# Sums of both attention layers: one-hots from a TensorE product of bit codes and one relu, in place of four Abs operations and a relu

## The chip, the core and the metric

The kernel runs on one core of a Trainium2 chip. The core has TensorE (matrix products, PE in the profile), VectorE (DVE), ScalarE (ACT), GpSimd (POOL) and SyncE (SP), which here only issues transfers. Each engine takes its own instructions in order and they meet through semaphores. The metric is device time in microseconds (us), as the median of several runs.

## The reference, cut to what matters

A graph of 6250 nodes with 106250 edges sorted by target `dst`, and four layers on it: a two-layer GATv2 attention network, two GCN-like convolutions and an edge network. The change touches the two attention layers:

```
def _gatv2_layer(x, src, dst, Wl, bl, Wr, br, att, bias, heads, out_ch, concat):
    xl = (x @ Wl + bl).reshape(N, heads, out_ch)
    xr = (x @ Wr + br).reshape(N, heads, out_ch)
    e = jax.nn.leaky_relu(xl[src] + xr[dst], NEG_SLOPE)
    logits = jnp.einsum('ehc,hc->eh', e, att)
    m = jax.ops.segment_max(logits, dst, num_segments=N)
    ex = jnp.exp(logits - m[dst])
    denom = jax.ops.segment_sum(ex, dst, num_segments=N)
    alpha = ex / denom[dst]
    msg = xl[src] * alpha[..., None]
    out = jax.ops.segment_sum(msg, dst, num_segments=N)
    ...
h = _gatv2_layer(x, src, dst, Wl1, ..., heads=8, out_ch=16, concat=True)    # layer 1: width 128
h = _gatv2_layer(h, src, dst, Wl2, ..., heads=1, out_ch=64, concat=False)   # layer 2: width 64
```

`segment_sum` over the edges of a target node is what the changed stage computes.

## The kernel before

Edges are cut into 880 tiles of 128, each belonging to one block of 128 target nodes; four tiles are a group, 220 groups in all. A sum over edges is a product: a one-hot matrix (edge by local target number) times the edges' rows. `LOCAL` holds each edge's local number, 0 to 127; an edge of another block has a number outside and must get a row of zeros.

Each attention layer (`gat_layer`) runs these stages, with a barrier of all engines behind each: `two_dense` (projections), `gat_logits` (POOL gathers four tiles a group into a ring of 12 groups, the logits are worked out, rows and logits are kept in DRAM), `edge_max` (running maxima) and `gat_sums`. Beside them POOL sends `merge` transfers, which fill an adjacency matrix for later layers; it issues a stated number of groups (`MERGES`) within each stage, so a barrier also waits for those.

`gat_sums` goes through the groups in a software pipeline written as a list of pieces with delays (`pipeline`, L120); it is unrolled, each engine gets its pieces in the order of the list, and rings of four slots (`RING`) and pairs of PSUM banks tie the engines to each other. For a group q:

- SP issues `fetch_max` (L2221: in layer 1 four transfers of 8 rows, in layer 2 one) and `fetch_rows` (L2230: the kept rows and logits). Before each it waits until its slot is free and increments a semaphore (`settle`).
- PE turns the maxima (`turn_max`, L2239), DVE subtracts them from the logits (`less_max`, L2270), ACT takes Exp (`exps`, L2255), DVE multiplies rows by it in two halves (`first_rows`, `last_rows`, L2282) and puts in the maximum of each segment's first edge (`first_max`, L2274).
- ACT makes the one-hots: `hots` (L2250) takes |row number - LOCAL| for each of four tiles, and at the end of `exps` (L2257) one Relu makes 1 - |.| of all four.
- PE multiplies (`products`, L2304: four f32 products, 144 columns wide), and DVE adds each into its block's accumulator (`Adder.tile`, L1151), interleaved with its other pieces.

Of the kernel before, what the change touches and what calls it, by code (L numbers as in the profile page):

```python
# [7 lines left out]
ALU = mybir.AluOpType  # L8
# [11 lines left out]
P = 128  # L20
# [7 lines left out]
GT = 4  # L28
# [21 lines left out]
UNITS = -(-NB // CB)  # L50
ABLK = 64
SPARE = ABLK - 1

CYCLE = NB - 1
LIGHT = 15
# [63 lines left out]
def pipeline(nc, pieces):  # L119


    most = max(late for _, late in pieces)

    def step(turn, u):
        for piece, late in pieces:
            slot = (u - late) % RING
            own = turn + (u - late - slot) // RING
            q = own * RING + slot
            if isinstance(q, int) and not 0 <= q < GROUPS:
                continue  # L130
            piece(q, slot, own)

    for t in range(GROUPS + most):
        step(t // RING, t % RING)


def gnn(nc, A, out):
    S = Sems(nc)
    ve, ac, pe, po, sp = nc.vector, nc.scalar, nc.tensor, nc.gpsimd, nc.sync
    with ExitStack() as ctx:  # L140
        def sb(name, shape, dt=F32):
            return ctx.enter_context(nc.sbuf_tensor(name, shape, dt))

        def dram(name, shape, dt=F32):
            return nc.dram_tensor(name, shape, dt).ap()
# [31 lines left out]
        CLASH = sb("CLASH", [1, FAR], I32)  # L177
        GIVEN = sb("GIVEN", [1, CYCLE], I32)
        zeros = sb("zeros", [P, CB * P])

        G = sb("G", [P, RING, GT, D + H1])
        OH = sb("OH", [P, 2, GT, P])
# [47 lines left out]
        def go(eng, f, by=1):  # L230
            chain[0].run(eng, f, by=by)
# [19 lines left out]
        def settle(eng, name):  # L251

            eng.sem_inc(S(f"settled_{name}"), 1)
# [12 lines left out]
        def fill(count, eng=ac):  # L266

            for _ in range(count):
                c, f = units_left.pop(0)
                w = min(CB, HEAVY - c * CB) * P  # L270
                eng.dma_start(adj[c, :, f * FILL:(f + 1) * FILL, 0:w],
                             zeros[:, 0:w].unsqueeze(1).broadcast_to([P, FILL, w])).then_inc(filled, 16)
# [17 lines left out]
            end()  # L290


        def sort_edges():

            begin()
# [15 lines left out]
                             ).then_inc(S("edges_copied"), 16)  # L311
            sp.wait_ge(chain[0].sem, chain[0].n)
            fill(FIRST[0], sp)
            go(ve, lambda: ve.tensor_copy(here[0:EP, 0:EC], here_i))
            go(ve, lambda: ve.tensor_copy(after[0:EP, 0:EC], after_i))

# [429 lines left out]
        def places_in_adjacency():  # L746

            begin()
            dst_c, bits = TOTAL[:, :].bitcast(I32), LATER[:, :].bitcast(I32)

            def put(source, right, keep, left):

                go(ve, lambda: ve.tensor_scalar(bits, source, right, keep, ALU.logical_shift_right, ALU.bitwise_and))
                go(ve, lambda: ve.tensor_scalar(bits, bits, left, None, ALU.logical_shift_left))
                go(ve, lambda: ve.tensor_tensor(PLACE[:, :], PLACE[:, :], bits, ALU.bitwise_or))

            wide_bits = (CB * P).bit_length() - 1
# [5 lines left out]
            clashes()  # L763
            ve.wait_ge(chain[0].sem, chain[0].n)

        def mean_and_root(halves, less_mean, root):
# [1080 lines left out]
        def gat_logits(tab, XR, H, C, half):  # L1847
# [30 lines left out]
            with ExitStack() as ps:  # L1878
# [173 lines left out]
                ve.wait_ge(S("masked"), 1)  # L2052
                if not half:
                    places_in_adjacency()
                pipeline(nc, [(gather_rows, 0), (fetch_locals, 0), (fetch_keys, 0), (fill_one, 0), (turned_hots, HOTS_LATE),
                              (pick, PICK_LATE), (add_rows, BEND_LATE), (scale_down, BEND_LATE), (twins, BEND_LATE),
                              (leaky, BEND_LATE), (weigh, BEND_LATE), (add_up, BEND_LATE), (turn_logits, TURN_LATE),
# [3 lines left out]
                po.wait_ge(S("aside"), 4)  # L2061
                po.wait_ge(filled, 16 * (len(UNIT_LIST) + 1 + HEAVY))
                merge(MERGES[half][0])
                for s in range(DEEP):
                    sp.wait_ge(S(f"kept{s}"), 16 * (-(-(GROUPS - s) // DEEP)))
                for s in range(LD):
# [130 lines left out]
        def gat_sums(acc, H, C, weights):  # L2197
# [13 lines left out]
            DIF = BUF[2][:, at + RING:at + 2 * RING, 0:TH].rearrange("p r (t h) -> p r t h", h=H)  # L2211
            by_group = head_d[0:H * TILES * P].rearrange("(h g t e) -> g t h e", h=H, t=GT, e=P)
            whole, R, LOGIT = ring(W, H)
            with ExitStack() as ps:
# [27 lines left out]
                def by_head(a):  # L2242
                    return a.rearrange("p (t h) -> p t h", h=H)

                def hots(q, slot, turn):
# [13 lines left out]

                def weight_column(q, slot, turn):  # L2260
                    if weights:
# [690 lines left out]
```

## Time and profile before

| | us |
|---|---|
| median of three runs (6759.13 to 6762.62) | 6760.27 |
| span of the profiled execution | 6773.4 |
| ... logits of layer 1, in that execution | 173 to 1280 |
| ... sums of layer 1 | 1426 to 1906 |
| ... sums of layer 2 | 3156 to 3567 |

Over the span PE is busy 71%, DVE 62%, ACT 32%, POOL 68%, but each stage has its own limit: in the chart of 40 slices, of 169 us each, ACT shows 8 and 9 tenths in the slices that lie within the sums of layer 1 and 9 in those of layer 2, against 4 or less in most others. The profile's chain of waits covers the last 1400 us alone, so the two stages have to be read from their timelines. Busy times of instructions that follow each other closely overlap: a rate is better read from the starts of two equal instructions in two turns of the loop.

### The profile page before, as it was taken

To read this page: it belongs to the slowest core of one execution; us is meant where nothing else is said; L and a number is where in the kernel's file an instruction comes from. 1 tells how busy PE (TensorE), PEld (TensorE's weight loads), DVE (VectorE), ACT (ScalarE), POOL (GpSimd) and SP (SyncE) were. 2 spreads that over 40 slices of the span, in tenths; PEclk is the share of its full clock that TensorE was granted. 3 is DMA by queue.
4 is the path that set the end of the run, shared out by engine and by line. 5 is a ranking of instruction groups with operands and counts; after the bars stand their busy time and mean duration, and the time that the engine had idled before them with its cause. 6 is when DMAs were issued, how large, how long until landed. Compare 5 with 4: busy or idle time off the path is not lost. (4 is left out here: it accounts for less than half of the span.)

```text
span 6773.4 us, 97374 instructions
## 1 busy us (share of the span) xinstructions
PE 4805.9 (71%) x22507; PEld 3515.7 (52%) x22507; DVE 4202.7 (62%) x13908; ACT 2200.1 (32%) x5456; POOL 4572.6 (68%) x4354
## 2 busy tenths in 40 slices
PE   3777765248776666443886996555555699999998
PEld 2444443136664444333776995555555455555555
DVE  7899985588976666335886445555555644344343
ACT  4444444268943333334993003111111300000000
POOL 1777777778857777777876662777777177276473
PEclk8555555578965555556998997776777799999999
DMA  5988865557744444333445884555555299899997
GB/s 202 305 285 290 275 184 146 111 101 138 144 80 106 107 106 99 81 80 47 76 76 151 286 284 137 156 152 150 150 151 149 58 299 306 289 304 295 299 305 256
DMA packets 896445, 1222.20 MB, mean 180 GB/s; under 512 B 229324, under 2 KB 633952, under 8 KB 882906
## 3 DMA queue, kind: packets, MB, share of 16 engines
q1 hardware_dynamic: 585406, 877.15, 40.3%
q0 software_dynamic: 206208, 217.12, 16.4%
q10 hardware_dynamic: 104268, 121.66, 5.4%
q8 instruction: 202, 3.31, 0.2%
q14 instruction: 361, 2.96, 0.1%
HBM read 979.26 MB, written 237.38 MB: 180 GB/s over the span
## 5 line engine op out<-in xcount | busy, mean ns | idle before, releaser
L1121 POOL DMA_INDIRECT ACC<-table,TABS x1760 | 1661.5, 944 | 610.1 <-issue 610.1
L1436 POOL DMA_INDIRECT BUF<-table,TABS x840 | 796.5, 948 | 600.7 <-issue 245.4
L1202 POOL DMA_INDIRECT adjacency<-TABS x600 | 964.1, 1607 | 305.5 <-issue 265.5
L1739 POOL DMA_INDIRECT TABS<-table,SPOT_SRC x836 | 841.1, 1006 | 317.8 <-issue 317.8
L1912 PE MATMUL picked<-BUF,G 128*128 x2368 | 597.0, 434 | 425.5 <-DVE ACC L1937 399.7
L1912 PEld LDWEIGHTS picked<-BUF,G 128*128 128x128 f32 x2368 | 527.0, 328 | 667.9 <-issue 667.9
L2304 PE MATMUL asum<-BUF 128*128 128x144 f32 x3520 | 563.5, 305 | 165.4 <-DVE BUF L2282 163.3
L1762 PE MATMUL pre<-wmat,BUF 128*128 128x128 f32 x1672 | 342.6, 369 | 469.5 <-DVE BUF L1772 435.8
L1920 DVE TENSOR_TENSOR picked<-picked,ACC 128x512 f32<-128x512 f32 (+1 forms) x440 | 247.6, 563 | 580.0 <-DMA ACC<-table,TABS 526.8
L2304 PEld LDWEIGHTS asum<-BUF 128*128 128x128 f32 x3520 | 478.5, 198 | 196.2 <-issue 179.3
L2250 ACT ACTIVATE BUF<-iota_row,TABS 128x128 f32<-128x128 f32 x1760 | 555.2, 386 | 23.0 <-PEq L95 23.0
L1762 PEld LDWEIGHTS pre<-wmat,BUF 128*128 128x128 f32 x1672 | 295.4, 266 | 514.3 <-issue 478.9
L1925 ACT ACTIVATE BUF<-picked 128x512 f32<-128x512 f32 (+1 forms) x440 | 215.6, 490 | 959.3 <-DVE picked L1920 958.8
L1151 DVE TENSOR_TENSOR ACC<-ACC,asum 128x144 f32 (+1 forms) x1760 | 462.0, 263 | 95.5 <-PE asum L2304 15.4
L1778 ACT ACTIVATE BUF<-BUF 128x512 f32<-128x512 f32 x209 | 131.8, 630 | 968.8 <-DVE BUF L1772 968.8
L1772 DVE TENSOR_TENSOR BUF<-pre,TABS 128x512 f32<-128x512 f32 x209 | 144.5, 691 | 485.8 <-DMA TABS<-table,SPOT_SRC 452.1
L1912 PE MATMUL picked<-BUF,OH 128*128 x1152 | 290.7, 434 | 215.4 <-DVE ACC L1937 215.4
L1912 PEld LDWEIGHTS picked<-BUF,OH 128*128 128x128 f32 x1152 | 256.5, 328 | 333.3 <-issue 333.3
L1567 DVE TENSOR_TENSOR BUF<-BUF,turned 128x128 f32 x560 | 161.0, 287 | 396.5 <-PE turned L1473 330.5
L1350 PE MATMUL sums<-ACC,BUF 128*128 128x128 f32 x3332 | 386.1, 276 | 23.1 <-DMA BUF<-adjacency 13.3
L1978 PE MATMUL wspread<-BUF,ones 1*128 1x512 f32 x300 | 306.2, 1122 | 123.6 <-DVE BUF L1999 114.2
L1350 PEld LDWEIGHTS sums<-ACC,BUF 128*128 128x128 f32 x3332 | 379.4, 193 | 24.8 <-DMA BUF<-adjacency 13.8
(431 smaller groups left out, 9802.7 us busy)
## 6 DMA issues: line engine op xcount, KB each, us to landing
TABS<-adjacency SPq DMA_DIRECT2D x272, 512.0 KB
BUF<-in_edge_pair SPq DMA_DIRECT2D x836, 128.0 KB
BUF<-adjacency SPq DMA_DIRECT2D x102, 1024.0 KB
BUF<-adjacency SPq DMA_DIRECT2D x204, 512.0 KB
adjacency<-zeros ACTq DMA_DIRECT2D x44, 1792.0 KB
G<-adjacency SPq DMA_DIRECT2D x136, 512.0 KB
kept<-ACC SPq DMA_DIRECT2D x220, 272.0 KB, 4.8
G<-kept SPq DMA_DIRECT2D x220, 272.0 KB
```

The costliest lines, as they stand in the source:

```text
L1121: po.indirect_dma_start(rows[:, slot, j, 0:width], None, tab, bass.IndirectOffsetOnAxis(ap=SRC[:, q * GT + j:q * GT + j + 1], axis=0)).the ...
L1151: ve.tensor_tensor(at, at, self.from_[:, j, 0:self.width], ALU.add).then_inc(S("added"), 1)
L1202: po.indirect_dma_start(adj_flat, bass.IndirectOffsetOnAxis(ap=PLACE[:, k:k + 1], axis=0), TOTAL[:, k:k + 1], None, compute_op=ALU.add).th ...
L1350: m = pe.matmul(sums[:, j, 0:P], RA[n % len(RA)][:, (i * w + j) * P:(i * w + j + 1) * P], xw[:, b + i, :], start=b + i == 0, stop=b + i == ...
L1436: po.indirect_dma_start(R[:, q % deep_ring, j, :], None, table, bass.IndirectOffsetOnAxis(ap=SRC[:, k:k + 1], axis=0)).then_inc(S(f"gather ...
L1739: po.indirect_dma_start(R[:, g % RD, j, :], None, table, bass.IndirectOffsetOnAxis(ap=SPOT_SRC[:, k:k + 1], axis=0)).then_inc(S(f"gathered ...
L1762: m = pe.matmul(pre[g % FREE][:, j, :], PAIR[:, g % PD, j, 0:D], wmat[:, :], start=True, stop=True)
L1912: m = pe.matmul(z, OHT[q % HD][:, j, :], XR[:, bass.ds(blocks[j], 1), 0:W].rearrange("p a d -> p (a d)"), start=True, stop=True)
L1920: ve.tensor_tensor(z, z, whole[:, q % DEEP, 0:GT * W], ALU.add).then_inc(S("summed"), 1)
L1978: pe.matmul(wspread[n % 2][:, :, :].rearrange("p t e -> p (t e)"), ones[P // 4 * (n % KD):P // 4 * (n % KD) + 1, :], WROW[n % KD].rearrang ...
L2250: ac.activation(HOT[:, slot, j, :], iota_row[:, :], ACT.Abs, scale=-1.0, bias=LOCAL[:, bass.ds(q * GT + j, 1)]).then_inc(S("gap"), 1)
L2304: m = pe.matmul(sums[slot % 2][:, j, 0:WIDE], HOT[:, slot, j, :], RHS[:, slot, j, :], start=True, stop=True)
```

## The change

Each edge's local number is turned once into a code of 8 values: seven of -0.5 or 0.5 for its bits and one that is -6 for an edge of this block and -16 otherwise. Each column has a code of seven times -2 or 2, and 1. The product of an edge's and a column's code is 7 - 6 = 1 where they agree, at most -1 where a bit differs, and negative for edges outside; a relu of it is the one-hot. A group of four tiles is one bf16 product: 32 rows of codes against a fixed 32 x 512 matrix (`COLUMNS`, four copies of the columns' codes on the diagonal).

```
+        CODES = sb("CODES", [P, 3, TTAB], BF16)
+        COLUMNS = sb("COLUMNS", [P, GT, P], BF16)
+        code_d = dram("codes", [TTAB, BITS, P], BF16)
...
+        def code_columns():            # in sort_edges, ahead of the first work on the loaded edges
+            ...
+            for b in range(BITS - 2, -1, -1):
+                own.run(ve, lambda: ve.tensor_scalar(bits[:, b:b + 1], left, float(P // 2), 0.5, ALU.is_ge, ALU.subtract))
+                own.run(ve, lambda: ve.scalar_tensor_tensor(left, bits[:, b:b + 1], -float(1 << b), left, ALU.mult, ALU.add))
+            ...
+                for t in range(GT):
+                    own.run(pe, lambda: pe.matmul(columns[0:CODE_ROWS, t, :], apart[:, t * CODE_ROWS:(t + 1) * CODE_ROWS],
+                                                  ident[:, :], start=True, stop=True))
+                own.run(ve, lambda: ve.tensor_copy(COLUMNS[0:CODE_ROWS, :, :], columns[0:CODE_ROWS, :, :]))
...
+        def codes_of_locals(left):     # in gat_logits of layer 1, ahead of its pipeline
+            rows = local_d.rearrange("(g p) e -> p g e", p=P)
+            sp.dma_start(left.rearrange("p (g e) -> p g e", g=TCOL), rows).then_inc(S("local_rows"), 16)
+            ...
+            for n, b in enumerate(range(BITS - 2, -1, -1)):
+                room = n % 3
+                if n > 1:
+                    ve.wait_ge(S(f"codes_stored{room}"), 16 * ((n + 1) // 3))
+                go(ve, lambda: ve.tensor_scalar(CODES[:, room, :], left, float(P // 2), 0.5, ALU.is_ge, ALU.subtract))
+                ...
+                if b:
+                    go(ve, lambda: ve.scalar_tensor_tensor(left, CODES[:, room, :], -float(1 << b), left, ALU.mult, ALU.add))
+            for b in stores:
+                ...
+                sp.dma_start(code_d.rearrange("(g p) b e -> b p g e", p=P)[b],
+                             CODES[:, room, :].rearrange("p (g e) -> p g e", g=TCOL)).then_inc(S(f"codes_stored{room}"), 16)
...
         # gat_sums
+                meets = [psum(ps, f"meets{i}", [P, GT, P]) for i in range(2)]
+                def fetch_codes(q, slot, turn):
+                    wait(sp, S("met"), q - CD + 1)
+                    settle(sp, "sync")
+                    sp.dma_start(coded[:, q % CD, :], code_d[q * GT:(q + 1) * GT].rearrange("t b e -> (t b) e")
+                                 ).then_inc(S(f"codes{q % CD}"), 16)
+                def meet(q, slot, turn):
+                    pe.wait_ge(S(f"codes{q % CD}"), 16 * (q // CD + 1))
+                    wait(pe, S("hot"), q - 1)
+                    pe.matmul(meets[slot % 2][:, :, :].rearrange("p t d -> p (t d)"), coded[:, q % CD, :],
+                              COLUMNS[0:CODE_ROWS, :, :].rearrange("p t d -> p (t d)"), start=True, stop=True
+                              ).then_inc(S("met"), 1)
                 def hots(q, slot, turn):
+                    ac.wait_ge(S("met"), q + 1)
                     wait(ac, S("summed"), q - RING + 1)
-                    for j in range(GT):
-                        ac.activation(HOT[:, slot, j, :], iota_row[:, :], ACT.Abs, scale=-1.0,
-                                      bias=LOCAL[:, bass.ds(q * GT + j, 1)]).then_inc(S("gap"), 1)
+                    ac.activation(HOT[:, slot], meets[slot % 2][:, :, :], ACT.Relu).then_inc(S("hot"), 1)
                 def exps(q, slot, turn):
                     ac.wait_ge(S("dif"), q + 1)
                     ac.activation(RHS[:, slot, :, W:W + H], DIF[:, slot], ACT.Exp).then_inc(S("exp"), 1)
-                    ac.wait_ge(S("gap"), (q + 1) * GT)
-                    ac.activation(HOT[:, slot], HOT[:, slot], ACT.Relu, scale=-1.0, bias=1.0
-                                  ).then_inc(S("hot"), 1)
...
-                pipeline(nc, [(fetch_max, 0), (fetch_rows, 1), (turn_max, 2), (ve_step(less_max), 2),
+                pipeline(nc, [(fetch_max, 0), (fetch_codes, 0), (fetch_rows, 1), (turn_max, 2), (meet, 2),
+                              (ve_step(less_max), 2),
                               (ve_step(first_rows), 3), (ve_step(first_max), 2), (ve_step(last_rows), 3),
                               (ve_step(weight_column), 2), (add, 5),
-                              (flush, 0), (hots, 2), (exps, 2), (products, 4)])
+                              (flush, 0), (exps, 2), (hots, 2), (products, 4)])
```

SP's queue in the middle of the sums of layer 1, before; L2227 is `fetch_max` and L2233 `fetch_rows`, and `pool` numbers are semaphores:

```order
L2233 DMA G<-kept 128x544 [waits pool6]
L2227 DMA BUF<-heads 8x128 [waits pool2]
L2227 DMA BUF<-heads 8x128 x3
L2233 DMA G<-kept 128x544 [waits pool6]
L2227 DMA BUF<-heads 8x128 [waits pool2]
L2227 DMA BUF<-heads 8x128 x3
```

And now, with L2293 and L2299 the same two pieces and L2315 `fetch_codes`:

```order
L2299 DMA G<-kept 128x544 [waits pool9]
L2293 DMA BUF<-heads 8x128 [waits pool2]
L2293 DMA BUF<-heads 8x128 x3
L2315 DMA CODES<-codes 32x128 [waits pool5]
L2299 DMA G<-kept 128x544 [waits pool9]
L2293 DMA BUF<-heads 8x128 [waits pool2]
L2293 DMA BUF<-heads 8x128 x3
L2315 DMA CODES<-codes 32x128 [waits pool5]
```

Each turn of the loop has a sixth transfer with a wait of its own, between the maxima and the rows.

PE's queue in the same place, before; `asum` is the product of one-hots and rows, `mcol` the turned maxima:

```order
L2239 MATMUL mcol_27<-ident,BUF 128x32 [waits pool10,pool16]
L2304 MATMUL asum_29<-BUF 128x144 [waits pool10,pool19,pool6,pool15]
L2304 MATMUL asum_29<-BUF 128x144 x3
L2239 MATMUL mcol_26<-ident,BUF 128x32 [waits pool10,pool4]
L2304 MATMUL asum_28<-BUF 128x144 [waits pool10,pool19,pool6,pool15]
```

And now, with L2305, L2322 and L2380 for `turn_max`, `meet` and `products`:

```order
L2305 MATMUL mcol_30<-ident,BUF 128x32 [waits pool14,pool19]
L2322 MATMUL meets_28<-COLUMNS,CODES 128x512 [waits pool15,pool27]
L2380 MATMUL asum_32<-BUF 128x144 [waits pool14,pool24,pool9,pool15]
L2380 MATMUL asum_32<-BUF 128x144 x3
L2305 MATMUL mcol_29<-ident,BUF 128x32 [waits pool14,pool4]
L2322 MATMUL meets_27<-COLUMNS,CODES 128x512 [waits pool15,pool6]
```

One product of 512 columns stands between the turned maxima and the four products of each group.

## Rows read from the trace of the kernel before

**Rows 1.** Busy time of each engine (and instructions) in the two sums stages

```profile
core 0: us, PE busy (x) PEld busy (x) DVE busy (x) ACT busy (x) POOL busy (x), PEclk, DMA share, GB/s
...
1426.00:1906.00 480.00, 370.38 (x2200) 318.30 (x2200) 434.11 (x1761) 422.79 (x1321) 361.62 (x224) 0.93 0.68 137
...
3156.00:3567.00 411.00, 338.78 (x2200) 293.84 (x2200) 341.62 (x1982) 402.74 (x1320) 325.73 (x208) 0.99 0.48 74
```

**Rows 2.** Timeline, one turn of the sums of layer 1: start, duration, engine

```profile
1649.11 0.30 DVE L1151 TENSOR_TENSOR ACC<-ACC,asum 128x144 f32 x1
...
1649.27 0.34 SPq L2233 DMA_DIRECT2D G<-kept  x1
1649.28 1.22 PE L2304 MATMUL asum<-BUF 128*128 128x144 f32 x8 [0.47 <-DVE BUF L2282]
...
1649.54 0.23 ACT L2255 ACTIVATE BUF<-BUF 128x32 f32<-128x32 f32 x1
...
1649.72 1.28 SPq L2227 DMA_DIRECT2D BUF<-heads  x4
...
1650.20 1.26 ACT L2250 ACTIVATE BUF<-iota_row,TABS 128x128 f32<-128x128 f32 x4
...
1650.43 0.40 PE L2239 MATMUL mcol<-ident,BUF 32*128 32x32 f32 x2
...
1651.12 0.30 DVE L1151 TENSOR_TENSOR ACC<-ACC,asum 128x144 f32 x1
...
1651.28 0.34 SPq L2233 DMA_DIRECT2D G<-kept  x1
```

**Rows 3.** Timeline, SP's queue at the start of the same stage

```profile
1426.31 2.84 SPq L2227 DMA_DIRECT2D BUF<-heads  x8
...
1429.71 1.28 SPq L2227 DMA_DIRECT2D BUF<-heads  x4
1431.10 0.34 SPq L2233 DMA_DIRECT2D G<-kept  x1
1431.55 1.28 SPq L2227 DMA_DIRECT2D BUF<-heads  x4
```

**Rows 4.** Timeline, SP's queue: a slow issue, and the last turns

```profile
1626.29 2.85 SPq L2227 DMA_DIRECT2D BUF<-heads  x4
...
1891.73 2.54 SPq L2233 DMA_DIRECT2D G<-kept  x2
```

**Rows 5.** Timeline, turns of the sums of layer 2

```profile
3401.10 1.22 PE L2304 MATMUL asum<-BUF 128*128 128x144 f32 x8 [0.42 <-DVE BUF L2282]
3401.18 0.22 DVE L1151 TENSOR_TENSOR ACC<-ACC,asum 128x67 f32 x1
...
3401.49 0.19 ACT L2255 ACTIVATE BUF<-BUF 128x4 f32<-128x4 f32 x1
...
3402.25 0.38 PE L2239 MATMUL mcol<-ident,BUF 4*128 4x4 f32 x2
...
3402.89 0.23 DVE L1151 TENSOR_TENSOR ACC<-ACC,asum 128x67 f32 x1
...
3403.33 0.19 ACT L2255 ACTIVATE BUF<-BUF 128x4 f32<-128x4 f32 x1
```

**Rows 6.** Timeline, POOL behind the barrier that ends the sums of layer 2

```profile
3569.20 1.56 POOL L1202 DMA_INDIRECT adjacency<-TABS  x1 [22.15 <-issue]
```

**Rows 7.** Timeline, SP's queue at the start of the sums of layer 2

```profile
3158.16 0.26 SPq L2224 DMA_DIRECT2D BUF<-heads  x1
```

**Rows 8.** Timeline, PE in a later stage: f32 products of 512 columns

```profile
5451.38 3.60 PE L1519 MATMUL sums<-BUF,ACC 128*128 128x512 f32 x8
```

**Rows 9.** Timeline, DVE in `sort_edges`: its first work on loaded edges

```profile
14.30 0.60 DVE L314 CAST BUF<-BUF 125x850 f32<-125x850 int32 x1 [9.56 <-DMA BUF<-in_dst]
```

**Rows 10.** Timeline, start of the logits of layer 1

```profile
173.36 0.95 POOL L1121 DMA_INDIRECT ACC<-table,TABS  x1 [69.70 <-issue]
...
175.45 1.09 DVE L755 TENSOR_TENSOR TABS<-TABS 128x896 int32<-128x896 int32 x1
...
184.09 0.20 DVE L1186 TENSOR_TENSOR GIVEN<-st 1x48 int32<-1x48 f32 x1
...
199.18 1.02 SPq L2038 DMA_DIRECT2D kept<-ACC  x1
```

More of the change, by code:

```diff
@@ L52 @@
 SPARE = ABLK - 1
+BITS = 8
+CODE_ROWS = GT * BITS
+CD = 8
 CYCLE = NB - 1
@@ L290, in constants @@
             end()
+        def code_columns():
+            own = Chain(S("columns"))
+            room = G[:, 0, :, :].rearrange("p t d -> p (t d)")
+            left, bits, apart = room[:, 0:1], room[:, 8:8 + BITS], room[:, 64:64 + GT * CODE_ROWS]
+            own.run(ve, lambda: ve.tensor_copy(left, iota_col[:, :]))
+            own.run(ve, lambda: ve.memset(bits, 0.0))
+            for b in range(BITS - 2, -1, -1):
+                own.run(ve, lambda: ve.tensor_scalar(bits[:, b:b + 1], left, float(P // 2), 0.5, ALU.is_ge, ALU.subtract))
+                own.run(ve, lambda: ve.scalar_tensor_tensor(left, bits[:, b:b + 1], -float(1 << b), left, ALU.mult, ALU.add))
+            own.run(ve, lambda: ve.tensor_scalar(bits, bits, 4.0, None, ALU.mult))
+            own.run(ve, lambda: ve.memset(bits[:, BITS - 1:BITS], 1.0))
+            own.run(ve, lambda: ve.memset(apart, 0.0))
+            for t in range(GT):
+                at = t * (CODE_ROWS + BITS)
+                own.run(ve, lambda: ve.tensor_copy(apart[:, at:at + BITS], bits))
+            with ExitStack() as ps:
+                columns = psum(ps, "columns", [P, GT, P])
+                for t in range(GT):
+                    own.run(pe, lambda: pe.matmul(columns[0:CODE_ROWS, t, :], apart[:, t * CODE_ROWS:(t + 1) * CODE_ROWS],
+                                                  ident[:, :], start=True, stop=True))
+                own.run(ve, lambda: ve.tensor_copy(COLUMNS[0:CODE_ROWS, :, :], columns[0:CODE_ROWS, :, :]))
         def sort_edges():
@@ L313, in sort_edges @@
             fill(FIRST[0], sp)
+            code_columns()
             go(ve, lambda: ve.tensor_copy(here[0:EP, 0:EC], here_i))
@@ L763, in places_in_adjacency @@
             clashes()
+            ve.wait_ge(chain[0].sem, chain[0].n)
+        def codes_of_locals(left):
+            rows = local_d.rearrange("(g p) e -> p g e", p=P)
+            sp.dma_start(left.rearrange("p (g e) -> p g e", g=TCOL), rows).then_inc(S("local_rows"), 16)
+            ve.wait_ge(S("local_rows"), 16)
+            after, valid = CODES[:, 0, :], CODES[:, 1, :]
+            go(ve, lambda: ve.tensor_scalar(after, left, 0.0, None, ALU.is_ge))
+            go(ve, lambda: ve.scalar_tensor_tensor(valid, left, float(P), after, ALU.is_lt, ALU.mult))
+            go(ve, lambda: ve.tensor_scalar(CODES[:, 2, :], valid, 10.0, -16.0, ALU.mult, ALU.add))
+            made = {BITS - 1: (2, chain[0].n)}
+            stores = [BITS - 1]
+            for n, b in enumerate(range(BITS - 2, -1, -1)):
[3 more added lines that the diff above has]
+                go(ve, lambda: ve.tensor_scalar(CODES[:, room, :], left, float(P // 2), 0.5, ALU.is_ge, ALU.subtract))
+                made[b] = (room, chain[0].n)
+                stores.append(b)
+                if b:
+                    go(ve, lambda: ve.scalar_tensor_tensor(left, CODES[:, room, :], -float(1 << b), left, ALU.mult, ALU.add))
+            for b in stores:
+                room, known = made[b]
+                sp.wait_ge(chain[0].sem, known)
+                settle(sp, "sync")
+                sp.dma_start(code_d.rearrange("(g p) b e -> b p g e", p=P)[b],
+                             CODES[:, room, :].rearrange("p (g e) -> p g e", g=TCOL)).then_inc(S(f"codes_stored{room}"), 16)
             ve.wait_ge(chain[0].sem, chain[0].n)
@@ L2054, in gat_logits @@
                     places_in_adjacency()
+                    codes_of_locals(JUNK[:, :, :, :].rearrange("p r t d -> p (r t d)")[:, 0:TTAB])
                 pipeline(nc, [(gather_rows, 0), (fetch_locals, 0), (fetch_keys, 0), (fill_one, 0), (turned_hots, HOTS_LATE),
@@ L2063, in gat_logits @@
                 merge(MERGES[half][0])
+                if not half:
+                    for room, stores in enumerate((3, 2, 3)):
+                        sp.wait_ge(S(f"codes_stored{room}"), 16 * stores)
                 for s in range(DEEP):
@@ L2213, in gat_sums @@
             whole, R, LOGIT = ring(W, H)
+            coded = CODES[:, :, :].rearrange("p r e -> p (r e)")[0:CODE_ROWS, 0:CD * P].rearrange(
+                "p (r e) -> p r e", r=CD)
             with ExitStack() as ps:
+                meets = [psum(ps, f"meets{i}", [P, GT, P]) for i in range(2)]
                 mcol = [psum(ps, f"mcol{i}", [P, 4 * P]) for i in range(2)]
@@ L2243, in by_head @@
                     return a.rearrange("p (t h) -> p t h", h=H)
+                def fetch_codes(q, slot, turn):
+                    wait(sp, S("met"), q - CD + 1)
+                    settle(sp, "sync")
+                    sp.dma_start(coded[:, q % CD, :], code_d[q * GT:(q + 1) * GT].rearrange("t b e -> (t b) e")
[6 more added lines that the diff above has]
+                              ).then_inc(S("met"), 1)
                 def hots(q, slot, turn):
+                    ac.wait_ge(S("met"), q + 1)
                     wait(ac, S("summed"), q - RING + 1)
-                    for j in range(GT):
-                        ac.activation(HOT[:, slot, j, :], iota_row[:, :], ACT.Abs, scale=-1.0,
-                                      bias=LOCAL[:, bass.ds(q * GT + j, 1)]).then_inc(S("gap"), 1)
+                    ac.activation(HOT[:, slot], meets[slot % 2][:, :, :], ACT.Relu).then_inc(S("hot"), 1)
                 def exps(q, slot, turn):
```

## The prediction

> **What bounds the kernel now.** The profile's chain of waits ends in the last layer and says nothing of these stages, so I took the busy times by stage first and then one turn of each loop. In the sums of layer 2 ACT is busy 402.7 of 411 us, in those of layer 1 422.8 of 480, where DVE has 434.1 [rows 1]. The reader is to see from the timeline which engine has no gap in a turn, by the distance between equal instructions.
>
> Layer 2: ACT's Exp starts at 3401.49 and again at 3403.33, a turn of 1.84 us. DVE's turn is shorter: its first add of a group starts at 3401.18 and 3402.89, which is 1.71 [rows 5]. It runs on until one of its multiplications finds the Exp not ready. So ACT sets the pace of layer 2.
>
> Layer 1: equal DVE adds stand at 1649.11 and 1651.12, a turn of 2.01 us that DVE fills with eight pieces; ACT (0.66 from Exp over Relu to the first Abs, then four Abs) needs the same 1.84 and so has 0.17 to spare; PE starts its products after a gap of 0.47 [rows 2]. DVE sets the pace, ACT only nearly. The third engine close to it is SP, which no busy time shows. Its own turn, when nothing holds it, is 1.84: from 1429.71 over 1431.10 to 1431.55 [rows 3], of which 1.28 are the four issues of maxima and 0.34 the issue of the rows. In the steady loop SP's turn is 2.01 as well (1649.27 to 1651.28), and from the end of its maxima (1649.72 + 1.28 = 1651.00) to the next rows 0.28 pass, against 0.11 when free [rows 2, 3]. SP's slack is thus 0.17 us in a turn, no more. The average turn of the stage is longer than the steady one: (1891.73 - 1426.31) / 219 = 2.12 [rows 3, 4]. Part is PE at half clock in short stretches (granted clock 0.93 over the stage [rows 1]), and part is slow issues on SP, such as four maxima in 2.85 instead of 1.28 [rows 4]; I count 34 turns with such an issue, together 14 us over the usual.
>
> **The change, part by part.** *ACT*, both layers: four Abs go, 1.84 - 0.66 = 1.18 of a turn [rows 2, 5], and a Relu of 128 x 512 stays, now from PSUM. ACT's turn falls to about 0.7. In layer 1 this was hidden behind DVE's 2.01 and is worth nothing in itself. In layer 2 it lifts the bound.
>
> *DVE* in the loops: no instruction comes or goes. Its turns of 2.01 and 1.71 stay.
>
> *SP* in the loops: one more transfer in each turn, of 32 rows of 256 bytes. Issues near it: 0.26 for 4 rows [rows 7], 0.32 for each of the four of 8 rows (1.28 / 4), 0.34 for the rows of a group, which fill 128 partitions [rows 3]. I take 0.31, bounds 0.26 and 0.34. It has a wait and a `settle` ahead, which cost 0.11 where the same pair stands today. So 0.42, bounds 0.37 and 0.46. In layer 2 SP needs 0.26 + 0.34 + 0.42 + two gaps of 0.11, or 1.24, and stays hidden. In layer 1 it needs 1.84 + 0.42 = 2.26, which is more than DVE's 2.01: SP becomes the bound. 219 turns of 2.26 are 495 us. The slow issues no longer hide in slack: 14 us, with six transfers for five some 16. 511 in place of 465.4, thus +46 us; the half clock of PE, which is now absorbed by rings that stay ahead, is the reason why I don't add its cost again. With the bounds of the issue +35 and +55. The tail behind the last transfer gets shorter by about 1 us, since the others follow SP closer: +45.
>
> The Trainium skill says in "Trainium Kernel Development and Optimization", Key Constraints, that issuing transfers from several engines only saves the sequencer's issue time, since all run on the same DMA engines. By that rule an added transfer of 8 KB costs this kernel its issue alone, and the sum above is of the right kind; the trace agrees in that the DMA share is 0.68 in this stage, not full [rows 1].
>
> *PE* in the loops: one bf16 product of 512 columns and 32 rows for each group. The trace has no bf16 product. From below, one of the eight records of a group's products, 144 columns, takes 0.14 (eight records fill the 1.15 from 3401.10 to 3402.25 [rows 5]). From above, an f32 record of 512 columns takes 0.43 (two starts 3.43 apart make eight; 3.60 with the last one's drain [rows 8]). I take 0.26, between them and nearer to the lower, since an f32 record of the same columns moves twice the bytes. Layer 1: turned maxima from 1650.43 to 1650.83, then a gap to 1651.29 [rows 2]; 0.26 fits in its 0.47, and even 0.43 does. In layer 2 PE has 1.15 for products and some 0.30 for the turned maxima, so 1.71 with the new product: level with DVE's 1.71. Together I take 1.75.
>
> The Trainium skill, "TensorE: Matmul & The Clock Gate", section Back-to-back issue gap, puts a bf16 product at one cycle for each column, 0.21 us for 512 at 2.4 GHz. An estimate by that page is a PE turn of 1.66 and a layer 2 bound by DVE at 1.71. No row here shows it.
>
> *Layer 2 as a whole*: 220 turns of 1.84 become 220 of 1.75, or 20 us less. But POOL has its own work in this stage, its 208 merge transfers [rows 1], and a barrier waits for it. It idles 22.15 us before its first transfer behind the barrier, some 2 of them the crossing [rows 6]; so no more than 20 can be won, whatever the engines do. Both limits lie close together, so I take -16, bounds -20 and, with a product of 0.43 and a PE turn of 1.88, +10.
>
> *`code_columns`*: about 27 small operations on DVE, each waiting for the one before, four products and a copy, all ahead of the cast that waits 9.56 us for loaded edges [rows 9]. I estimate 8 us, from the 0.2 to 0.25 that dependent small operations take at a time (L1186 and its neighbours [rows 10]) and some 0.7 for each product: hidden, +0 to +2 us; I take +1.
>
> *`codes_of_locals`*: 16 operations of 896 columns, at most 1.09 each [rows 10], behind the places (end 184.3), and waits for rooms that are still being stored; about 20 us, and SP's queue holds its first fetches of locals behind the stores of the codes. All of the logits' loop starts 20 us later, but POOL sets that stage: one gather each 1.25 us, 12 groups ahead, so it meets a full ring only at 173.4 + 48 x 1.25 = 233. The first `kept` is issued at 199.2 [rows 10] and would be at about 220, landing by 225. Nothing is lost; the cover is gone if the delay exceeds 30 us.
>
> *Sum*: +45 - 16 + 1 + 0 = +30 us, on the profiled execution's 6773.4 us of span 6803. That execution is 13 us above the median of the runs, which is no part of these stages that I can name, so I put the difference on the median: 6790 us.
>
> **The rivals.**
> *A, SP has room.* The new issue might be cheaper than its neighbours, or overlap with its wait, and SP's turn stay under 2.01. For it: SP waits in most turns today. Against it: its slack is 0.17 and the cheapest issue in reach is 0.26 without its wait. Then layer 1 stays as it is, perhaps a few us better where ACT's lag behind the half clock goes, and layer 2 gives its 16: 6760 - 16 + 1 = 6745, faster.
> *B, PE becomes the bound of layer 2.* If the new product costs 0.43 as the f32 record does, PE's turn there is 1.88 and layer 2 gains nothing but loses 10; layer 1 still pays 45: 6760 + 45 + 10 + 1 = 6816. It decides from 0.39 upwards (1.15 + 0.30 + 0.39 = 1.84). For it: `meet` is in order ahead of the products. Against it: bf16.
> *C, the new start of the logits isn't hidden.* DMA share is high there, the stores of the codes have small rows, and each third one is waited for. If the delay is 50 us instead of 20, POOL stands still for 20: 6810.
> *D, PE falls to half clock in layer 1 more often.* It idles 2.26 - 1.15 - 0.30 - 0.26 = 0.55 of a turn, as today (2.01 - 1.15 - 0.30 = 0.56), and today most of the stage is granted 2.4 GHz (0.93 [rows 1]). At 1.2 GHz its turn would be twice 1.71, or 3.4 us; a fifth of the turns there adds 0.2 x 219 x 1.1, some 50: 6840.
>
> **How the numbers follow.** Forecast 0.58, A 0.16, B 0.12, C 0.08, D 0.06. The forecast's own range is 6772 (issue 0.26, layer 2 at -20, slow issues half absorbed) to 6808. Down to A's 6745 and up past B's 6816 to 6824 the range leaves out the better half of A and most of D. A measurement of this kernel tells no less than 0.2%, or 13.5 us, from no change. Faster by more than that: most of A, 0.14. Same: the rest of A and the lower edge of the forecast, 0.12. Slower: 0.74.
>
> **What would show it.** Right: in the sums of layer 1 equal issues of the rows on SP stand 2.26 apart, with no gap in SP's turn longer than 0.12, and DVE waits for the DMA of kept rows or maxima in each turn; the stage ends some 45 us later. In layer 2 the turn is 1.71 to 1.76, ACT is busy under half of it, and POOL's idle time before the barrier is 2 to 6 us in place of 22. The product of codes takes 0.2 to 0.3. DVE's cast of loaded edges still starts at 14 to 16, and POOL's gathers in the logits stay 1.25 apart. Wrong: SP still waits for DVE in layer 1 (A), PE without a gap in layer 2 (B), a gap between gathers near 233 (C), a granted clock under 0.85 in layer 1 (D).

## The result and the profile after

The changed kernel takes 7295.4 us (median of 4 runs, 7291.2 to 7306.9) against 6760.7 for the kernel before on the same chip: the ratio is 1.079 [1.078, 1.081]. The prediction was 6790 with a range to 6824. The direction was right, the size wrong by more than ten times: +535 us in place of +30.

Both stages that the change touches grew, and nothing else did. The length of a stage is taken from DVE's clearing of the accumulator to DVE's first instruction behind the stage.

| us | before | after |
|---|---|---|
| start of the sums of layer 1 | 1427.8 | 1431.2 |
| sums of layer 1 | 478.4 | 714.2 |
| between the two sums | 1251.5 | 1251.8 |
| sums of layer 2 | 410.2 | 704.9 |
| behind them, to the end of the span | 3205.5 | 3190.0 |

The last line holds nothing that was changed; its 15 us come for the most part from the profiled execution of before, 13 us over the median, in which this part is the longest; in those of all other kernels below it takes 3187 to 3200. Busy times of the same stages in the kernel after, which answer to [rows 1]:

```profile
core 0: us, PE busy (x) PEld busy (x) DVE busy (x) ACT busy (x) POOL busy (x), PEclk, DMA share, GB/s
1431.00:2145.00 714.00, 704.35 (x2420) 541.60 (x2420) 446.61 (x1761) 157.68 (x440) 351.32 (x224) 0.50 0.46 95
3397.00:4102.00 705.00, 699.09 (x2420) 542.63 (x2420) 331.08 (x1982) 160.84 (x440) 325.62 (x208) 0.50 0.29 46
```

Read the third number from the right first: the granted clock is 0.50, that is 1.2 GHz, from end to end in both stages. It was 0.93 and 0.99. PE is busy 704 of 714 us and 699 of 705: it sets the pace of both layers. ACT's busy time did fall, from 423 and 403 to 158 and 161, and is worth nothing. In the middle of the stages, where no start and no end is counted in, PE has no gap at all:

```profile
1500.00:1800.00 300.00, 300.00 (x1030) 230.42 (x1030) 187.17 (x749) 67.08 (x188) 251.10 (x161) 0.50 0.55 96
3500.00:3800.00 300.00, 300.00 (x1040) 232.60 (x1038) 140.87 (x846) 68.75 (x188) 239.88 (x154) 0.50 0.38 47
```

PE's part of the timeline in layer 1, to be held against [rows 2]:

```profile
1702.31 0.63 PE L2305 MATMUL mcol<-ident,BUF 32*128 32x32 f32 x2
1702.76 0.61 PE L2322 MATMUL meets<-COLUMNS,CODES 32*128 32x512 bf16 x1
1703.30 2.29 PE L2380 MATMUL asum<-BUF 128*128 128x144 f32 x8
1705.52 0.63 PE L2305 MATMUL mcol<-ident,BUF 32*128 32x32 f32 x2
1705.96 0.61 PE L2322 MATMUL meets<-COLUMNS,CODES 32*128 32x512 bf16 x1
```

From one pair of turned maxima to the next are 3.21 us: 0.45 turned maxima, 0.54 codes, 2.22 products. Before, the same group's products took 1.15 from start to start and the turn was 2.01. The new product is only 0.54 of the 1.20 us by which the turn grew; the rest is the old work at half clock. Layer 2 has the same turn: its products start at 3600.03 and 3603.21.

```profile
3600.03 2.29 PE L2380 MATMUL asum<-BUF 128*128 128x144 f32 x8
...
3602.86 0.23 DVE L1210 TENSOR_TENSOR ACC<-ACC,asum 128x67 f32 x1 [1.57 <-PE asum L2380]
3603.00 0.15 DVE L2346 TENSOR_TENSOR BUF<-G,mcol 128x4 f32<-128x4 f32 x1
3603.18 0.21 ACT L2334 ACTIVATE BUF<-BUF 128x4 f32<-128x4 f32 x1 [2.45 <-DVE BUF L2346]
3603.21 1.09 PE L2380 MATMUL asum<-BUF 128*128 128x144 f32 x3
```

DVE waits 1.57 for the products and ACT 2.45 for DVE; PE waits for nobody. 219 turns of 3.2 are 701 us, nearly the whole of the 705 and 714 that the stages take.

The rest of the prediction can be read off as well. SP's free turn at the start of layer 1 (against [rows 3]), from one issue of rows to the next:

```profile
1436.10 0.36 SPq L2299 DMA_DIRECT2D G<-kept  x1
1436.56 1.28 SPq L2293 DMA_DIRECT2D BUF<-heads  x4
1437.94 0.31 SPq L2315 DMA_DIRECT2D CODES<-codes  x1
1438.36 0.36 SPq L2299 DMA_DIRECT2D G<-kept  x1
```

It is 2.26, as computed, with the new issue at 0.31. At a PE turn of 3.2 it doesn't matter.

### The profile page after: what moved, and what is told of

It is laid out like the page before. It is cut to its first block and busy times, and to the rows that moved or that the text cites. A ratio compares the mean times of both kernels' runs of the same rounds, so it can differ in the third digit from the quotient of the medians.

```text
span 7292.1 us, 98323 instructions
## 1 busy us (share of the span) xinstructions
PE 5487.1 (75%) x22955; PEld 3979.7 (55%) x22955; DVE 4220.1 (58%) x13948; ACT 1694.4 (23%) x3696; POOL 4563.0 (63%) x4354
## 5 line engine op out<-in xcount | busy, mean ns | idle before, releaser
L2380 PE MATMUL asum<-BUF 128*128 128x144 f32 x3520 | 1004.1, 467 | 2.7 <-DVE BUF L2358 1.6
L2380 PEld LDWEIGHTS asum<-BUF 128*128 128x128 f32 x3520 | 852.6, 330 | 199.3 <-issue 196.8
L1313 POOL DMA_INDIRECT G<-table,TABS x280 | 275.6, 984 | 130.4 <-issue 96.6
```

The costliest lines, as they stand in the source:

```text
L1313: po.indirect_dma_start(R[:, q % RING, j, :], None, table, bass.IndirectOffsetOnAxis(ap=SRC[:, q * GT + j:q * GT + j + 1], axis=0)).then_i ...
L2380: m = pe.matmul(sums[slot % 2][:, j, 0:WIDE], HOT[:, slot, j, :], RHS[:, slot, j, :], start=True, stop=True)
```

## The experiments

A product's rows are here those over which it sums, 32 for the codes; in a profile line they are the first number of `32*128`. Theory: an added product that has few rows holds TensorE at 1.2 GHz, whatever its busy time. The rivals are that the product costs its time and PE is simply full; that the clock needs a better start; and that SP's added transfer does the harm. The table has all runs; "clock" is the mean of the whole execution (0.745 in the profiled one of before), the lengths are those of the profiled execution. Each ratio is to runs of the kernel before on the same chip, whose medians lie between 6755.4 and 6765.8. "One run" is a single execution; 15 executions of the kernel before, in one series, spread over 22 us, so a single run tells 7284 from 6746 but not 6770 or 6746 from 6760.

| kernel | us | ratio to before | clock | sums 1 | sums 2 |
|---|---|---|---|---|---|
| before | 6760.7 | | 0.745 | 478.4 | 410.2 |
| after | 7295.4 | 1.079 [1.078, 1.081] | 0.675 | 714.2 | 704.9 |
| rows128 | 6810.5 | 1.008 [1.006, 1.009] | 0.749 | 540.7 | 397.2 |
| before_x32 | 7284.4 | one run | 0.676 | 713.2 | 703.8 |
| before_x64 | 7329.4 | one run | 0.677 | 735.5 | 723.2 |
| before_x72 | 6746.3 | one run | 0.749 | 461.3 | 410.4 |
| before_x96 | 6750.5 | one run | 0.753 | 462.0 | 410.3 |
| before_x128 | 6746.1 | one run | 0.751 | 463.4 | 410.3 |
| before_x128_timed | 6745.2 | 0.998 [0.997, 0.999] | 0.749 | 461.2 | 410.3 |
| before_x32c128 | 7156.4 | one run | 0.675 | 642.8 | 634.0 |
| before_f32x32 | 7366.5 | one run | 0.673 | 747.9 | 744.2 |
| before_x32small | 6770.0 | one run | 0.745 | 478.0 | 410.3 |
| warm | 6999.6 | one run | 0.712 | 717.3 | 402.6 |
| before_fetch | 6821.4 | 1.009 [1.007, 1.010] | 0.742 | 533.5 | 410.3 |
| act_fetch | 6739.6 | 0.996 [0.995, 0.997] | 0.753 | 461.0 | 395.5 |
| hybrid | 6734.5 | 0.995 [0.994, 0.997] | 0.751 | 462.5 | 395.7 |

**rows128.** The changed kernel with the same product over all 128 rows; the rows from 32 on are zeros in both operands.

```
-pe.matmul(meets[slot % 2]..., coded[:, q % CD, :], COLUMNS[0:CODE_ROWS, :, :]...)
+pe.matmul(meets[slot % 2]..., coded_all[:, q % CD, :], COLUMNS[:, :, :]...)
```

> The changed kernel, but the product of codes takes all 128 rows: the rows 32 to 127 of both operands are zeros, so it computes the same. Theory 1 (rows): TensorE's clock stays at 1.2 GHz because the product of 32 rows keeps TensorE busy for long and counts for little; with 128 rows the clock rises to 2.4 GHz some 10 us into each sums stage, as in the kernel before, and the time is what I forecast with a 2.4 GHz clock, 6770 to 6810. Theory 2 (any product): every further product of 512 columns in the turn does it, whatever its rows: 7295, granted clock 0.50 in both stages. Theory 3 (other parts of the change: new waits on SP and ACT): 7295 too.

Zeros in 96 rows win 485 us, and theories 2 and 3 fall. The 6810.5 lie at the upper edge of what theory 1 was given. The busy times by stage:

```profile
1434.00:1975.00 541.00, 444.96 (x2420) 346.67 (x2420) 440.44 (x1762) 158.52 (x440) 353.18 (x224) 0.91 0.62 125
3230.00:3627.00 397.00, 386.13 (x2418) 317.40 (x2417) 333.51 (x1983) 152.76 (x440) 325.34 (x208) 0.98 0.52 82
```

The clock is nearly back at what it was. Layer 2 is now shorter than before by 13.0; layer 1 is longer by 62.3, for the most part the term of SP (below).

**before_x32 and before_x128.** The kernel before with one more bf16 product in each turn, behind the turned maxima, of 32 or of 128 rows and 512 columns; nothing reads its result.

```
+def extra_product(q, slot, turn):
+    pe.matmul(extra...[:, 0:512], source[0:32, 0:P], source[0:32, 512:512 + 512], start=True, stop=True)
```

> The kernel before with one bf16 product of 32 rows and 512 columns more in each turn of both sums stages, behind the turned maxima; it waits for nothing, nobody waits for it, and its result isn't used. Theory 1 (rows) and theory 2 (any product): the clock stays at 1.2 GHz, the turn is 3.2 us in layer 1 and 3.0 or more in layer 2, in all 7230 to 7300. Theory 3 (the new waits or transfers): clock as before, layer 1 as before, layer 2 0 to 10 us longer, 6760 to 6775.

> The same as before_x32 with 128 rows in the added product. Theory 1: the clock rises as in the kernel before, perhaps with fewer falls in layer 1; 6750 to 6775. Theory 2: as before_x32, 7230 to 7300. Theory 3: 6760 to 6775.

> The kernel before with an unused bf16 product of 128 rows x 512 columns in every turn, timed this time. One look gave 6746 us with both stages at 2.4 GHz nearly throughout, layer 1's sums in 463.4 us in place of 478.4, layer 2's unchanged at 410.3. If the removal of the clock's dips in layer 1 is real, the ratio is 0.998 (about -14 us) and the interval ends below 1.000; if the dips were chance of one execution, the ratio is 1.000 and layer 1 as long as in the kernel before.

PE's timeline of before_x32 in layer 1:

```profile
1700.45 2.29 PE L2310 MATMUL asum<-BUF 128*128 128x144 f32 x8
1702.67 0.63 PE L2241 MATMUL mcol<-ident,BUF 32*128 32x32 f32 x2
1703.12 0.61 PE L2245 MATMUL extra<-beyond 32*128 32x512 bf16 x1
1703.66 0.61 PE L2310 MATMUL asum<-BUF 128*128 128x144 f32 x1
```

This is the turn of the changed kernel to the hundredth, with all the Abs operations, without a transfer of codes, without a code table. The product alone carries the loss. With 128 rows the same product makes the kernel not slower but a little faster (before_x128_timed, 0.998).

**before_x64, before_x96, before_x72.** The same with other numbers of rows (`source[0:64, ...]` and so on).

> The kernel before with the unused product over 64 rows (512 columns). Theory 1 (rows): somewhere between 32 rows (clock stays at 1.2 GHz, 7284) and 128 rows (6746). If only rows beside the work already there matter, at 1.2 GHz the turn is 3.2 us as with 32 rows, and the result shows on which side 64 rows fall: about 6750, or about 7284, or layer 2 alone at 2.4 GHz, about 6990.

> The kernel before with an unused bf16 product of 96 rows x 512 columns in every turn of both sums. 32 and 64 rows held TensorE at 1.2 GHz (7284 and 7329 us), 128 rows held it at 2.4 GHz (6746 us). If only products that fill the array's rows count: 0.50 in both stages and about 7300 us. If the rows add up, three quarters of them should be enough for most of the time: over 0.8 and under 6900 us. I hold the second slightly more likely.

> The kernel before with an unused bf16 product of 72 rows x 512 columns in every turn of both sums. 64 rows gave 7329 us at 1.2 GHz, 96 rows 6750 us at 2.4 GHz. If the switch lies between what fits in half the array's rows and what doesn't: 72 rows behave as 96 do, both stages at 1.00, 6740 to 6760 us. If the rows count by their number and the switch lies somewhere between 64 and 96: mixed or 0.50, over 6900 us. I hold the first at 60 in 100.

One stretch of layer 1 from each of 64 and 72 rows:

```profile
1500.00:1800.00 300.00, 300.00 (x997) 229.66 (x997) 181.69 (x728) 174.06 (x545) 250.60 (x160) 0.50 0.53 91
```

```profile
1500.00:1800.00 300.00, 274.41 (x1612) 208.29 (x1613) 283.45 (x1172) 280.71 (x879) 250.93 (x155) 1.00 0.73 146
```

Eight rows more, and 583 us less. In 300 us PE does 1612 pieces of work in place of 997 and still has 26 us to spare. (The 45 us between 32 and 64 rows are a turn of 3.31 in place of 3.21, at the same clock.) The Trainium skill, "TensorEngine Tiling (Array Packing)", Performance Considerations, names row tiling for a contraction of at most 64 rows: two row tiles at 64, four at 32. The switch that these runs show lies between 64 and 72 rows, where that use ends; that the tiling is its cause no run shows.

**before_x32c128, before_f32x32, before_x32small.** What else about the product matters: a bf16 product of 32 rows with 128 columns, an f32 product of 32 rows and 128 columns, and a bf16 one of 32 rows and 4 columns.

```
x32c128:  source[0:32, 0:P] by source[0:32, 512:512 + 128]      (bf16)
f32x32:   beyond[0:32, 0, :] by beyond[0:32, 1, :]              (f32, 128 columns)
x32small: source[0:32, 0:P] by source[0:32, 512:512 + 4]        (bf16)
```

> The kernel before with an unused bf16 product of 32 rows and only 128 columns in every turn of both sums, so a quarter of the length of the product that by itself took the kernel to 7284 us. If it is the mere presence of a product with few rows that holds TensorE at 1.2 GHz: granted clock 0.50 in both stages, some 7150 to 7250 us. If it is the share of time spent in such products (32 rows x 512 columns were 0.60 us of a 3.2 us turn; these would be 0.15 of 2.8 at 1.2 GHz): the clock stays mostly at 2.4 GHz, perhaps with more dips than in the kernel before (0.91 in layer 1), 6750 to 6850 us.

> The kernel before with an unused f32 product of 32 rows x 128 columns in every turn of both sums, which takes TensorE about as long as a bf16 product of 512 columns. The kernel before has four f32 products of 4 rows and 4 columns in every turn (turned maxima) and yet reaches 2.4 GHz, so few rows alone are not enough for the loss. If few rows over many columns do it whatever the type: granted clock 0.50, some 7280 us. If it is the bf16 type together with few rows: the clock stays at about 0.9 to 1.0, 6740 to 6800 us.

> The kernel before with an unused bf16 product of 32 rows x 4 columns in every turn of both sums. 128 columns gave 7156 us and 512 columns 7284 us, both at 0.50 throughout. If any bf16 product of few rows holds the clock down: 0.50 in both stages, some 7100 us. If it takes a certain share of columns: the clock is that of the kernel before, 0.91 and more, 6750 to 6790 us. I hold the second at 60 in 100, since the four f32 products of 4 x 4 do no harm.

One stretch of each layer, first of before_x32c128, then of before_f32x32, then of before_x32small, whose second stretch is an earlier one because its layer 2 ends at 3570:

```profile
1500.00:1800.00 300.00, 300.00 (x1145) 256.31 (x1145) 207.66 (x833) 199.18 (x625) 251.32 (x156) 0.50 0.58 104
3500.00:3800.00 300.00, 300.00 (x1156) 258.67 (x1155) 156.78 (x945) 198.69 (x630) 177.68 (x114) 0.50 0.33 49
```

```profile
1500.00:1800.00 300.00, 300.00 (x1071) 255.29 (x1069) 178.46 (x712) 170.82 (x535) 250.71 (x161) 0.50 0.53 89
3500.00:3800.00 300.00, 300.00 (x1071) 255.13 (x1070) 132.62 (x804) 168.79 (x536) 251.23 (x161) 0.50 0.37 41
```

```profile
1500.00:1800.00 300.00, 236.16 (x1551) 205.35 (x1551) 274.55 (x1131) 270.65 (x849) 252.25 (x156) 0.94 0.71 141
3200.00:3500.00 300.00, 254.81 (x1806) 220.84 (x1807) 252.27 (x1480) 300.00 (x985) 250.08 (x161) 1.00 0.50 76
```

The type is not it: f32 does the same harm. A fourth of the columns does the same harm too, so for before_x32c128 the first of its two expectations came true and the second, that a short product would be let through, fell. With 4 columns the stages are as before, although TensorE changes from 128 rows to 32 and back just as often: that change by itself does not hold the clock down. The turned maxima of the kernel before had misled me. They are products of few rows too, 32 rows by 32 columns in layer 1 and 4 by 4 in layer 2 (the expectations speak of 4 by 4 alone), and were there all along, at a clock of 0.93 and 0.99.

**warm.** The changed kernel with 12 f32 products of 128 rows and 512 columns ahead of each stage's loop.

```
+for _ in range(12):
+    pe.matmul(meets[1]..., ident[:, :], beyond[:, :, :]..., start=True, stop=True)
```

> The changed kernel with twelve dense f32 products (128 rows, 512 columns, result not used) on TensorE at the start of each sums stage, some 20 us at 1.2 GHz. If the loop only lacks a start (at 2.4 GHz its own turns would keep the clock up), the clock is 0.9 or more in both stages and the time 6790 to 6850. If the loop's mix can't keep the clock (theory 1 in its strict form), it falls back within some us: 7290 to 7330.

Stretches of both stages:

```profile
1430.00:1450.00 20.00, 17.53 (x59) 9.08 (x58) 10.51 (x22) 2.83 (x9) 16.71 (x11) 0.89 0.49 79
1450.00:1500.00 50.00, 49.58 (x175) 38.05 (x174) 32.13 (x130) 11.59 (x34) 41.99 (x27) 0.52 0.60 106
1500.00:1800.00 300.00, 300.00 (x1031) 231.01 (x1030) 187.83 (x750) 67.00 (x187) 251.12 (x161) 0.50 0.56 96
3400.00:3420.00 20.00, 19.56 (x75) 10.84 (x74) 8.65 (x42) 4.04 (x12) 16.65 (x12) 0.90 0.39 57
3500.00:3800.00 300.00, 293.17 (x1867) 227.95 (x1865) 255.19 (x1532) 116.23 (x337) 242.17 (x155) 1.00 0.51 82
```

PE in layer 1 where the clock falls:

```profile
1447.00 0.38 PE L2322 MATMUL meets<-COLUMNS,CODES 32*128 32x512 bf16 x1
1449.43 1.22 PE L2380 MATMUL asum<-BUF 128*128 128x144 f32 x8 [2.06 <-DVE BUF L2358]
...
1451.62 2.26 PE L2380 MATMUL asum<-BUF 128*128 128x144 f32 x8 [0.42 <-DVE BUF L2358]
```

Both layers are started near 2.4 GHz. In layer 1 PE then idles for 2.06 and 0.42 us, waiting for DVE, and at 1451.62 a group's products take 2.26 in place of 1.22: the clock has fallen. It never returns, though PE is busy without a gap from 1500 on. Layer 2 keeps 2.4 GHz to its end, with no wait of PE longer than 0.4 and with the same 32-row product that otherwise holds it at 1.2: for it both clocks are stable, and the start decides. So neither expectation held for both layers, the first came true in layer 2 and the second in layer 1. The few rows do not forbid the clock outright; they keep it from rising. That they also bring it down is not shown: in layer 1 it fell behind a wait, and it falls now and then in the kernel before as well (0.92 from 1500 to 1800), but comes back there. Whether layer 1, whose turned maxima are larger, could keep it without that wait was not tried.

**before_fetch.** The kernel before with the added transfer of 8 KB a turn on SP's queue alone, for a test of my own term.

```
+def fetch_more(q, slot, turn):
+    ...
+    sp.dma_start(FETCHED[0:32, q % 8, :], local_d[q % 27 * 32:q % 27 * 32 + 32])
```

> The kernel before with only the added transfer: in each turn of both sums stages SP fetches 32 rows of 256 bytes more, behind the maxima, with a wait and a settle ahead; nobody uses them. If SP's issue time is the second cost of the change (rows128 took 541 us for the sums of layer 1 against 478), SP's turn is 2.26 to 2.28 with no slack, the stage 530 to 540 us, the sums of layer 2 unchanged at 410, in all 6805 to 6820. If the loss of rows128 in layer 1 came from the product or from the new order on ACT, this runs in 6755 to 6765.

SP's queue in layer 1:

```profile
1697.56 0.35 SPq L2234 DMA_DIRECT2D G<-kept  x1
1698.02 1.28 SPq L2228 DMA_DIRECT2D BUF<-heads  x4
1699.41 0.31 SPq L2246 DMA_DIRECT2D FETCHED<-locals  x1
1699.84 0.35 SPq L2234 DMA_DIRECT2D G<-kept  x1
```

A turn of 2.28 with no gap over 0.12: SP is the bound, as the prediction had it. The stage grew by 55.1 to 533.5, as expected here (the prediction had 45 for this term); layer 2 didn't change. The total of 6821.4 is 1 us over its range.

**act_fetch.** rows128 with the fetch of the codes issued by ACT, which has had time since the Abs operations went.

```
-wait(sp, S("met"), q - CD + 1); settle(sp, "sync");   sp.dma_start(coded[:, q % CD, :], ...)
+wait(ac, S("met"), q - CD + 1); settle(ac, "scalar"); ac.dma_start(coded[:, q % CD, :], ...)
```

> rows128 with the codes' transfer issued by ACT's queue in place of SP's. If SP's issue time is the whole loss of layer 1, its turn goes back to DVE's 2.01 and the stage to 463 to 480 us; layer 2 stays at 397; set-up costs 6 more: in all 6730 to 6750. If ACT's issue delays the Exp that DVE waits for, layer 1 stays above 500 and the total above 6770.

The first expectation came true: layer 1 takes 461.0, 2 under its range, and layer 2 395.5. PE in layer 2:

```profile
3300.47 0.38 PE L2307 MATMUL mcol<-ident,BUF 4*128 4x4 f32 x2
3300.79 0.39 PE L2326 MATMUL meets<-COLUMNS,CODES 128*128 128x512 bf16 x1
3301.04 1.22 PE L2384 MATMUL asum<-BUF 128*128 128x144 f32 x8
3302.18 0.38 PE L2307 MATMUL mcol<-ident,BUF 4*128 4x4 f32 x2
```

**hybrid.** Layer 1 makes its one-hots as before, with an unused full-row product in each turn; layer 2 makes them from the codes over 128 rows.

> Layer 1 with Abs and Relu as in the kernel before, plus one unused bf16 product of 128 rows and 512 columns in each turn; layer 2 with codes over 128 rows. Layer 1 463 us as in before_x128 (the added product keeps the clock at 2.4 GHz), layer 2 397 as in rows128, set-up +6: 6730 to 6745, faster than both kernels. If the gain of before_x128 was chance, layer 1 takes 478 and the total is 6745 to 6755.

Both of the last two beat the kernel before, by 0.4 and 0.5%; their intervals overlap. The gain has two parts that can be told apart. Layer 2 wins 14.7 and 14.5 us by ACT's lifted turn. Layer 1 wins 17.4 and 15.9, which needs no codes: before_x128_timed, with all four Abs in place, wins 17.2 there. The stretch from 1500 to 1800 in the kernel before and in before_x128_timed:

```profile
1500.00:1800.00 300.00, 237.75 (x1400) 204.60 (x1400) 272.41 (x1121) 268.80 (x842) 252.09 (x157) 0.92 0.71 139
```

```profile
1500.00:1800.00 300.00, 274.54 (x1614) 208.37 (x1614) 283.51 (x1173) 280.87 (x880) 252.03 (x155) 1.00 0.72 146
```

The dips of the clock are gone, and DVE, which bounds this stage, gets 1173 instructions through in place of 1121.

## Why the prediction was wrong

**The step that failed** is the one on PE in the loops. For layer 1 it says "0.26 fits in its 0.47, and even 0.43 does", and for layer 2 it gives PE 1.71 with the new product. Every duration in it, that of the old products too ("one of the eight records of a group's products, 144 columns, takes 0.14"), is one at 2.4 GHz, and that the clock stays there rests on nothing but PE's idle time, which rival D found to be as before. At that clock the sizes were right: with 128 rows, in act_fetch, the product takes 0.25 (3300.79 to 3301.04) and PE's turn in layer 2 is 1.71 (3300.47 to 3302.18); with 32 rows, in layer 2 of warm, the turn is 1.72. What the product does to the clock was missing. Measured, the clock is 0.50 and PE's turn 3.21, and this gives +236 in layer 1 and +295 in layer 2 in place of +45 and -16. before_x32, rows128 and the step from 64 to 72 rows show that it is the few rows of the product; why few rows have this effect on the clock no run shows.

**Rival D** had the right mechanism, a fall to half clock, with the wrong driver, place and size. It looked for the cause in the share of time that PE idles, found it unchanged, and priced a fifth of the turns of layer 1 at +50. Its sign, a clock under 0.85 in layer 1, did show. The runs show the contrary: PE idles nowhere and is at 1.2 GHz. A busier engine was granted less. The Trainium skill, "TensorE: Matmul & The Clock Gate", What's actually happening, says that the clock is set by how busy the engine has been, and that sustained work brings 2.4 GHz. Here 300 of 300 busy us at 0.50, for hundreds of us, disagree; the measurement decides.

**The range** was bounded by the nearest rows for the product, 0.14 and 0.43. Both ends came from products of 128 rows, and the new one has 32. The bounds of a new instruction should have covered what it does to its neighbours too.

A row of the kernel before could have raised the doubt. It is from the logits' stage, where products of 1 row and 512 columns take 81.6 of PE's 290.6 busy us. The stretch from 300 to 700, by busy time, and then the row of these products in it:

```profile
300.00:700.00 400.00, 290.59 (x885) 177.19 (x883) 359.56 (x965) 175.33 (x322) 302.31 (x321) 0.50 0.87 288
```

```profile
L1978 PE MATMUL wspread<-BUF,ones 1*128 1x512 f32 x80 | 81.6, 1121 | 46.2 <-DVE BUF L1999 43.3 <-DVE BUF L1995 2.8
```

PE is busy for 73% there and yet at 0.50, while the sums of layer 1 have 370 of 480, 77%, at 0.93 [rows 1]. Whether the thin products are what holds that stage at 1.2 GHz wasn't tried.

**Layer 1 at full clock.** SP as the bound: right (2.26 forecast, 2.26 to 2.28 measured). The stage costs +62 in rows128 and +55 in before_fetch, against +45: about 4 us are the turn of 2.28 (219 x 0.02), the rest of the difference isn't explained by the runs. The clock is 0.84 from 1500 to 1800 in before_fetch, where PE waits more, so its dips are perhaps not absorbed as I took them to be; that is argued, not shown.

**Layer 2 at full clock.** -16 forecast, -13.0 to -14.7 measured. POOL's idle time before the barrier's end falls from 22.15 [rows 6] to 7.52 in act_fetch; I had said 2 to 6.

**`code_columns`.** The cast of loaded edges was the cover:

```profile
14.63 0.60 DVE L344 CAST BUF<-BUF 125x850 f32<-125x850 int32 x1 [1.31 <-DMA BUF<-in_dst]
```

It starts 0.33 later and has waited 1.31 in place of 9.56 [rows 9]: 8.25 us of work hidden, where I had estimated 8. Nothing of it is left where the logits begin: their first gather starts at 173.40 in place of 173.36.

**`codes_of_locals`.** POOL doesn't stand still, so C fell. The first `kept` was forecast at about 220:

```profile
216.60 1.54 SPq L2097 DMA_DIRECT2D kept<-ACC  x1
```

POOL's gathers from 190 to 600 wait 0.3 us for that transfer and are as many as before (328 against 329). But "nothing is lost" isn't quite so. From the first to the last of the 880 gathers pass 1101.7 us in place of 1098.0, and with it the sums of layer 1 start 3.4 later. It is 1101.4 to 1103.5 in the five kernels with codes and 1098.0 to 1099.5 in all those without. The slowest gather takes 1.85 in place of 1.47; what slows it wasn't tried.

**Rivals A and B** fell: SP had no room, and PE bounds layer 2 not by a product of 0.43 but by the clock.

## What to carry to other kernels

Before a product with few rows is put into a loop that lives on TensorE's 2.4 GHz, price all of TensorE's work in the loop at 1.2 GHz as well, or fill the product up to 128 rows with zeros: layer 2 took 397 us with them, 403 with 32 rows at full clock, 705 with 32 rows at half clock. When work moves from one engine to another, its transfer has an issuing engine too; give it to the engine that the change has relieved (layer 1 takes 540.7 with the fetch on SP and 461.0 with it on ACT; part of this is the clock, 0.90 and 1.00 from 1500 to 1800). And in the profile read the granted clock beside the busy share: an engine that is busy throughout at 0.50 may be the bottleneck by its clock and not by its load.

## What the runs showed of the hardware

- With an unused product of 32 or 64 rows and 512 columns in each turn, the granted clock of both stages is 0.50 for over 700 us each, at a PE that is hardly ever idle once the loop runs (300 of 300 us in the stretches shown); with 72, 96 or 128 rows it is 1.00 nearly throughout. At 32 rows f32 does the same as bf16, 128 columns the same as 512, and 4 columns do nothing. Rows of zeros count as rows (rows128: 0.91 and 0.98).
- The clock of a loop can be stable at both levels: in layer 2 of warm twelve dense products ahead of the loop decide for the 400 us behind them (402.6 in place of 704.9).
- Work that nothing needs can make a kernel faster: an unused 128-row product in each turn removes the clock's dips in layer 1 and 0.2% of the time (0.998, interval 0.997 to 0.999).
- A transfer of 32 rows of 256 bytes costs SP's queue 0.31 us for its issue and 0.11 for what stands ahead of it.
